# A fused block of attention and quantised feed-forward layers on one core: two VectorE operations, the seam between its halves, and its end are set to other places

## The reference, cut to what matters

```python
x = x + attn_a(layernorm(x))   # 16 heads, 64 wide; gelu; adds its own input too
x = x + ffn(layernorm(x))      # 256 -> 1024 -> relu -> 256, weights quantised to -1, 0, 1
x = x + attn_b(layernorm(x))   # 16 heads, 16 wide, rotary embedding, biases
x = x + ffn(layernorm(x))      # same weights
```

## Time and profile before

| what | us |
|---|---|
| median of 3 runs (3780.09 to 3784.66) | 3782.32 |
| profiled execution, its own time | 3781.21 |
| profiled execution, span from first to last instruction | 3779.0 |
| PE busy | 3626.6 |
| DVE busy | 2584.8 |
| ACT busy | 2385.9 |
| POOL busy | 1888.6 |

### The profile page before, as it was taken

How to read it: one execution, slowest core, us unless ns; L and a number is a source line. 1 busy time by engine, 2 the same in 40 slices (tenths; PEclk the granted TensorE clock), 3 DMA queues, 4 the chain that set the end, 5 groups by cost and what they waited for, 6 DMA issues and landing times.

```text
span 3779.0 us, 64440 instructions
## 1 busy us (share of the span) xinstructions
PE 3626.6 (96%) x23810; PEld 2433.1 (64%) x23810; DVE 2584.8 (68%) x4296; ACT 2385.9 (63%) x4629; POOL 1888.6 (50%) x1337
## 2 busy tenths in 40 slices
PE   8999999999999999999999978999999999999987
PEld 6777777777777777777777664555555555555534
DVE  6766666666667666666767656777777777777763
ACT  5665656556566566655656546777777777777754
POOL 4555555556555555555654633444444444444412
PEclk9999999999999999999999998999999999999989
DMA  2000000000000000000000012222222222222220
GB/s 79 7 12 1 12 12 12 1 12 12 1 12 12 1 12 12 9 5 12 12 1 15 25 43 47 53 62 62 63 62 61 61 63 58 62 59 64 53 48 18
DMA packets 102329, 116.27 MB, mean 31 GB/s; under 512 B 23557, under 2 KB 75269, under 8 KB 102021
## 3 DMA queue, kind: packets, MB, share of 16 engines
q1 hardware_dynamic: 102020, 112.17, 12.0%
HBM read 34.48 MB, written 27.26 MB: 16 GB/s over the span
## 4 chain that ended last, share of the span: by engine, by line
PE 76%; DVE 11%; ACT 7%; issue 5%; POOL 1%; DMA 0%; DVEq 0%; ACTq 0%; SPq 0%
PE ps_o L675 12%; PE ps_s L644 10%; PE ps_t L657 8%; PE ps_t L226 8%; PE ps_m L657 4%; PE ps_o L751 4%; PE ps_t L233 4%; DVE max_b L1160 4%; PE ps_t L786 4%; PE ps_m L226 3%; PE ps_t L710 3%; PE ps_s L724 3%; ACT et L867 2%; PE ps_m L233 2%; PE ps_s L738 2%
## 5 line engine op out<-in xcount | busy, mean ns | idle before, releaser
L534 POOL TENSOR_TENSOR e_a<-e_a,recip 128x1024 f32<-128x1024 f32 x512 | 969.4, 1894 | 948.7 <-DVE recip L1027 948.5
L825 ACT ACTIVATE e_a<-ps_s,neg_max 128x512 f32<-128x512 f32 x1024 | 695.1, 685 | 544.8 <-DVE neg_max L1020 544.4
L1160 DVE TENSOR_REDUCE max_b<-ps_s 128x2 f32<-128x1024 f32 x512 | 625.0, 1221 | 270.6 <-PE ps_s L724 268.8
L867 ACT ACTIVATE et<-ps_s 128x1024 f32<-128x1024 f32 x512 | 527.4, 1030 | 319.9 <-PE ps_s L738 319.0
L1020 DVE TENSOR_REDUCE neg_max<-ps_s 128x2 f32<-128x1024 f32 x512 | 623.0, 1217 | 67.7 <-PE ps_s L644 67.7
L675 PE MATMUL ps_o<-et_a,v_a 128*64 128x256 f32 x4096 | 499.8, 386 | 9.1 <-DVE heads_a L1063 4.8
L644 PE MATMUL ps_s<-raw_a 64*128 64x512 f32 x3072 | 425.9, 409 | 5.5 <-ACT e_a L825 5.3
L675 PEld LDWEIGHTS ps_o<-et_a,v_a 128*64 128x64 f32 x4096 | 279.2, 137 | 192.1 <-issue 78.3
L657 PE MATMUL ps_t<-ident,e_a 128*128 128x128 f32 x2660 | 394.0, 280 | 2.1 <-DVE xl L1219 2.0
L1034 DVE COPY et_a<-ps_t 128x512 f32<-128x512 f32 x366 | 251.1, 688 | 206.3 <-PE ps_t L657 202.1
L657 PEld LDWEIGHTS ps_t<-ident,e_a 128*128 128x128 f32 x2660 | 290.1, 141 | 133.2 <-issue 129.3
(11 more groups left out here) (194 smaller groups left out, 7231.0 us busy)
## 6 DMA issues: line engine op xcount, KB each, us to landing
q_stack<-roped_q SPq DMA_DIRECT2D x256, 96.0 KB
k_stack<-roped_k SPq DMA_DIRECT2D x256, 96.0 KB
x_a<-X SPq DMA_DIRECT2D x16, 512.0 KB, 3.4
X<-x_a SPq DMA_DIRECT2D x16, 512.0 KB, 2.9
x_ahead<-X SPq DMA_DIRECT2D x16, 512.0 KB, 3.8
X<-x_ahead SPq DMA_DIRECT2D x16, 512.0 KB, 2.9
x_before<-X SPq DMA_DIRECT2D x16, 512.0 KB, 3.9
OUT<-x_before SPq DMA_DIRECT2D x16, 512.0 KB, 5.2
```

What stands on the lines that cost most here:

```text
L534: nc.gpsimd.tensor_tensor(e_a[:, u % 5, :, :], e_a[:, u % 5, :, :], factor, ALU.mult).then_inc(e_normed, 1)
L825: ins = nc.scalar.activation(e_a[:, u % 5, h, :], ps_s[:, 2 * (u % 2) + h, :], ACT.Exp, bias=neg_max[:, u % 5, h:h + 1], accum_out=sums[:, ...
L867: nc.scalar.activation(et[:, v % 5, :, :], ps_s[:, 2:4, :], ACT.Exp)\
L1160: nc.vector.reduce_max(max_b[:, u // 4 % 2, :, u % 4], ps_s[:, score_bank(u):score_bank(u) + 2, :], AX.X, negate=True).then_inc(max_done, 1)
```

## The change: what it does

1. **Two VectorE operations, every sequence.** `LOWS[1]` (the second `roped_q`) goes from r = -26 to r = -24, behind the maximum of the next slot. In ffn1's norm the first `statistics` goes from r = 103 to 107, the second from 108 to 109, `aggregate` from 109 to 110. In the frame of one sequence, r = -24 is r = 104 of the sequence two before, so these stand side by side on DVE.
2. **End.** ffn1 of the last but one sequence (s = 14), with its output product, norm and bias, is set some 5 to 20 steps earlier, into the last scores of s = 15, and its save from r = 152 to r = 130.
3. **Seam.** x of sequence 1 goes to `x_before` instead of `x_ahead`; `load_second` loads it at slot 503, under a semaphore of its own, instead of after sequence 0's save. Its first norm and transposes are 4 to 12 steps earlier. The last heads' casts and low parts are two slots earlier, their product is at slots 528 and 529 instead of 536 to 538, in front of sequence 0's attn transposes, and the save of x is at 535 instead of 540.
4. **Transposes.** The first transpose of a norm waits for each 128-token piece of `xn` by itself and no longer for all four.

```diff
-        POST, LAST_POSTS = ((32, 32, 35, 36), (43, 44, 51, 52)), (56, 57, 58, 58)
+        POST, LAST_POSTS = ((32, 32, 35, 36), (43, 44, 51, 52)), (48, 48, 49, 49)
-        RESIDUAL, LOAD_X, SAVE_X, LAST_SAVE = 13, -22, 54, 60
+        RESIDUAL, LOAD_X, SAVE_X, LAST_SAVE = 13, -22, 54, 55
...
-                        if table[half][k] + late(s, half) == slot - UNITS * s:
+                        sooner = 2 if table is HEADS_HIGH and late(s, half) else 0
+                        if table[half][k] + late(s, half) - sooner == slot - UNITS * s:
...
-        NORM = {"ffn0": (-101, -100, -98, -93, -91), "attn": (-67, -64, -63, -51, -49), "ffn1": (103, 108, 109, 113, 115)}
+        NORM = {"ffn0": (-101, -100, -98, -93, -91), "attn": (-67, -64, -63, -51, -49), "ffn1": (107, 109, 110, 113, 115)}
+        WO_EARLY, XT_EARLY, FFN_EARLY = (95.5, 96.5, 98.5, 99.5), (107.1, 108.1), (99, 101, 102, 104, 105)
+        UP_EARLY, DOWN_EARLY = (110.1, 111, 112, 113.5, 115, 116.5, 118, 119), (121.5, 123.5, 125.5, 127)
+        BIAS_EARLY, SAVE_EARLY = 107, 130
+        XT_RAMP, FFN_RAMP = (-93.9, -92.9), (-109, -108, -107, -104, -103)
-        ROTATE, HIGHS, LOWS = (-39, -37, -35, -34, -32, -30), (-31, -29, -23, -21), (-28, -26, -20, -18)
+        ROTATE, HIGHS, LOWS = (-39, -37, -35, -34, -32, -30), (-31, -29, -23, -21), (-28, -24, -20, -18)
...
-        x_of = {"ffn0": x_ahead, "attn": x_ahead, "ffn1": x_before}
+        def x_of(part, s):
+            return x_before if part == "ffn1" or s == 1 else x_ahead
...
+                def load_second():
+                    sp.wait_ge(a_x_out, 16 * 2)
+                    sp.dma_start(x_before[:, :, :], X1[1, :, :].rearrange("(t p) d -> p t d", p=P)).then_inc(second_in, 16)
...
-                        pe.wait_ge(xn_ready, TB * (nth_norm[part, s] + 1))
                         for t in range(TB):
+                            if i == 0:
+                                pe.wait_ge(xn_ready, TB * nth_norm[part, s] + t + 1)
```

More of the change, by code:

```diff
@@ L158, in hybrid_block_kernel @@
         x_in = sem("x_in")
+        second_in = sem("second_in")
         a_x_out = sem("a_x_out")
@@ L320, in hybrid_block_kernel @@
         for s in range(BATCH):
-            plan += [(XT0[k], "transpose", "ffn0", k, s) for k in range(KT)]
+            plan += [((XT_RAMP if s == 1 else XT0)[k], "transpose", "ffn0", k, s) for k in range(KT)]
             plan += [((UP_RAMP if s == 1 else UP0)[f], "up", "ffn0", f, s) for f in range(FT)]
@@ L326, in hybrid_block_kernel @@
             plan += [(VB[t], "v", "attn", t, s) for t in range(TB)]
[L327 to L330, removed]
+            early = s == BATCH - 2
+            plan += [((WO_EARLY if early else WO1)[t], "wo", "ffn1", t, s) for t in range(TB)]
+            plan += [((XT_EARLY if early else XT1)[k], "transpose", "ffn1", k, s) for k in range(KT)]
+            plan += [((UP_EARLY if early else UP1)[f], "up", "ffn1", f, s) for f in range(FT)]
+            plan += [((DOWN_EARLY if early else DOWN1)[t], "down", "ffn1", t, s) for t in range(TB)]
         plan = sorted((SLOT * s + at_step, kind, part, i, s) for at_step, kind, part, i, s in plan)
@@ L354, in norm_at @@
         def norm_at(part, s):
-            return ATTN_RAMP if (part, s) == ("attn", 1) else NORM[part]
+            if (part, s) == ("ffn0", 1):
+                return FFN_RAMP
+            if (part, s) == ("attn", 1):
+                return ATTN_RAMP
+            return FFN_EARLY if (part, s) == ("ffn1", BATCH - 2) else NORM[part]
         norms = sorted((SLOT * s + norm_at(part, s)[0], part, s) for s in range(BATCH) for part in NORM)
@@ L434, in save_ahead @@
                     sp.wait_ge(biased, nth_norm["attn", s] + 1)
-                    sp.dma_start(X1[s, :, :].rearrange("(t p) d -> p t d", p=P), x_ahead[:, :, :]).then_inc(x_saved, 16)
+                    sp.dma_start(X1[s, :, :].rearrange("(t p) d -> p t d", p=P), x_of("attn", s)[:, :, :]).then_inc(x_saved, 16)
                 def load_before(s):
-                    sp.wait_ge(x_saved, 16 * (s + 1))
+                    sp.wait_ge(x_saved, 16 * max(s + 1, 2))
                     if s:
@@ L507, in _ @@
                         load_rest()
+                        load_second()
                     if slot == KEY_ONES:
@@ L512, in _ @@
                             r = step - SLOT * s
-                            if r == -108:
+                            if r == -108 and s != 1:
                                 load_ahead(s)
@@ L524, in _ @@
                                 load_before(s)
-                            if r == 152:
+                            if r == (SAVE_EARLY if s == BATCH - 2 else 152):
                                 save_before(s)
@@ L562, in add_bias @@
                         pool.wait_ge(weights_in, 8 * 16)
-                    nc.gpsimd.tensor_tensor(x_of[part][:, :, :], x_of[part][:, :, :],
+                    nc.gpsimd.tensor_tensor(x_of(part, s)[:, :, :], x_of(part, s)[:, :, :],
                                             rows_of(bo_rows if part == "attn" else b2_rows), ALU.add).then_inc(biased, 1)
@@ L620, in _ @@
                             for part in NORM:
-                                if r == BIAS[part]:
+                                if r == (BIAS_EARLY if (part, s) == ("ffn1", BATCH - 2) else BIAS[part]):
                                     add_bias(part, s)
@@ L874, in normalise @@
                     for t in (first, first + 1):
-                        nc.scalar.activation(xn[:, t, :], x_of[part][:, t, :], ACT.Identity, scale=rstd[:, t:t + 1],
+                        nc.scalar.activation(xn[:, t, :], x_of(part, s)[:, t, :], ACT.Identity, scale=rstd[:, t:t + 1],
                                              bias=shift[:, t:t + 1]).then_inc(xn_ready, 1)
@@ L1115, in statistics @@
                 def statistics(part, s, t):
-                    if part == "ffn0":
-                        dve.wait_ge(x_in, 16 * (s + 1))
+                    if part == "ffn0" and s == 1:
+                        dve.wait_ge(second_in, 16)
+                    elif part == "ffn0":
+                        dve.wait_ge(x_in, 16 * max(s, 1))
                     else:
@@ L1121, in statistics @@
                     for t in (t, t + 1):
-                        ins = nc.vector.bn_stats(stats[:, t, :], x_of[part][:, t, :])
+                        ins = nc.vector.bn_stats(stats[:, t, :], x_of(part, s)[:, t, :])
                     ins.then_inc(stats_ready, 1)
@@ L1135, in normalise @@
                     for t in (first, first + 1):
-                        nc.vector.tensor_scalar(xn[:, t, :], x_of[part][:, t, :], mean_var[:, t, 0:1], rstd[:, t:t + 1],
+                        nc.vector.tensor_scalar(xn[:, t, :], x_of(part, s)[:, t, :], mean_var[:, t, 0:1], rstd[:, t:t + 1],
                                                 ALU.subtract, ALU.mult).then_inc(xn_ready, 1)
@@ L1184, in empty @@
                         wait_filled(dve, fill)
-                        x = x_of[part][:, i - 1:i + 1, :]
+                        x = x_of(part, s)[:, i - 1:i + 1, :]
                         emptied(nc.vector.tensor_tensor(x, x, both, ALU.add), fill)
```

## The result

The kernel after takes 3836.9 us (median of 4 runs, 3833.8 to 3837.9), the kernel before, run beside it, 3783.5 us. The ratio is 1.014, 95% interval [1.0122, 1.0157]: 53 us slower, between 46 and 59. The forecast was 3805 us, 22 us slower: the sign was right, the size less than half.

What follows compares the result with a forecast made beforehand. TensorE, VectorE and ScalarE were taken to bound each sequence in turn, as a relay. 3781.2 + 29.5 (hold) + 4 (clock) - 8.3 (seam) - 2.0 (end) = 3804.4, plus 1.1 for the median: 3805.5 us; range 3774 to 3820.

Steps and rivals of the forecast that it cites:

- The held operation: Second `roped_q`, held on VectorE by GpSimd's ffn0 bias add: 2.11 us a sequence, 29.5 us over 14.
- the hold: Second `roped_q` ends at 3319.86, 0.55 us after GpSimd's add, instead of 3317.99: 1.87 us a sequence.
- the new place of `roped_q`: With `roped_q` moved away, VectorE waits for `xh` before `xl`: 0.24 us a sequence.
- The norm's later steps: ffn1's `statistics` and `aggregate` cost nothing new: power comes 1.1 us before `xn` needs it, VectorE being late.
- the relay: Within a sequence, whatever delays the last `roped_k` delays ScalarE's stretch, and TensorE's behind it, by the same amount.
- a port shared by halves: Alternative to full exclusion at `roped_q`: it loses another 0.6 us, 0.84 a sequence, 12 us in all.
- The clock: TensorE's idle time before the late maximum lowers the clock in about half of 13 sequences: 4 us, ends 0 and 21.
- the clock falls in every sequence: Rival: TensorE's doubled idle time lowers the clock in all 13 sequences, 21 us instead of 4: 3822; chance 0.05 above 3820.
- The seam: Last heads' products fill TensorE's idle time before the transposes; with 0.8 at sequence 1's norm, 8.3 us gained.
- The end: Twelve products moved into the last scores -0.3, x's earlier arrival -0.9, transposes -0.8: -2.0 us, ends -4.7 and +0.7.
- The sum: Whole kernel: 3781.2 + 29.5 + 4 - 8.3 - 2.0 = 3804.4, median 3805.5 us, 0.6% slower.

Runs made afterwards that it cites:

- the added products: Kernel after, with eight added 128x512 products per sequence where TensorE waits for the late maximum: 3818.5 us, ratio 1.0084.
- The three kernels with another end: Kernel before with the early end alone (3792.0 us), plus x in the other buffer (3786.4), plus two added products behind each of the last ten turned scores (3787.3).
- the two seam kernels: Kernel after with `LOWS`, `NORM` and end as before: 3785.6 us; the same with the last heads' low parts two slots earlier too: 3780.2 us.

## Why the prediction was right in sign and wrong in size

**The held operation: right.** The place (3317.40 for 3317.39), the duration (2.47 us, forecast 2.4 to 2.5), the end 0.55 us after GpSimd's, and the price once the clock is taken out (1.96 us a sequence, forecast 2.11) all hold. Term by term, the hold cost 1.75 us where 1.87 stood and the new place of `roped_q` 0.06 where 0.24 stood. The norm's later steps, which the prediction put at nothing because VectorE would be the late one at `xn`, cost 0.15: in that the reading failed, with GpSimd's power the late one. The runs with the add one step earlier and with `roped_q` back show it to be the cause. That the relay hands it on in full holds too; only the way is another, through TensorE's wait for the maximum and ScalarE's for scores.

The Trainium skill (SBUF — State Buffer, "Who interferes with whom") lets a VectorE instruction with two SBUF inputs and a GpSimd instruction that reads SBUF exclude each other. The trace agrees: 2.47 us beside the add, 0.68 us clear of it, where a port shared by halves would have given 1.2.

**The clock: the step that failed most.** The prediction said: "With more idle time I expect it in about half, at less than 1.6 us each", and took 4 us. The 2.4 us of idle time were forecast (2.36 measured), but not what they do: the clock fell in 13 of 13 sequences, at 1.22 us each, which is 15.9 us. The rival that had this, "the clock falls in every sequence", had the count right, with 1.6 us each, and gave 3822 us, still 15 short. What misled was one fall in 13 sequences, read as a chance of the edge to be scaled up. Eight falls in 13 with a hold of 2.05 us, 13 with 2.46 show how steeply it goes. The Trainium skill (TensorE: Matmul & The Clock Gate, "What's actually happening") lets the clock fall after idle time, and I named it for that rival; the falls came after TensorE's 2.36 us of idle time and 12 of 13 went when the added products left 0.51.

By traces, hold and clock make 14 x 1.96 + 13 x 1.22 = 43.3 us, and from the second `roped_q` of sequence 1 to that of sequence 15 the kernel after takes 43.6 us more than the kernel before. The two timed kernels that differ in `roped_q` alone are 45 us apart by their medians and 48 by their ratios. What lies between is within what such a difference is uncertain by.

**The seam: wrong.** "Their input is there in time ... casts and low parts need four operations of 1.3 us" failed. I counted four operations and did not place them: the casts move, the low parts do not, and the fourth stands behind the power in GpSimd's queue. The forecast was -8.3 us; measured are +1.1 (-2.3 to +4.5). With the low parts moved it is -5.3. Why it is not -8.3 stays open. Counted from the same `h_lo` in front of the seam (2201.67 before, 2204.70 with the low parts moved), the transposes start only 0.3 us later than before, so the idle time did take the four products. But the first stacked keys leave 3.4 us earlier, where 7.5 were forecast.

**The end: wrong in sign.** -2.0 us forecast, +7.2 measured (3.8 to 10.2), above the upper end of +0.7. The step said that x "no longer arrives at 3744.5 behind a load of 5.05 us" and looked at the load of s = 15 only. The earlier output product of s = 14 needs a load too, and that one waits for a save out of its buffer: 5.7 us of the 7.2 went with the other buffer. The low clock of the last slots was in the forecast, and was there (0.63 of full). How much of the 5.7 us is the clock, and what it costs by itself, the runs do not part.

**The sum.** Hold and clock +43 to +48 where 33.5 stood, seam +1 where -8.3 stood, end +7 where -2.0 stood: each of the three terms missed by 9 to 15 us and all to the same side. The single kernels add up to 56 us, the change is 53.

## What to carry to other kernels

When an operation with two SBUF inputs is moved, look up what GpSimd does at its new minute and which of the two could go first; here one step of a bias add was worth 43 us. Count the idle time that a delay leaves on TensorE, for that can cost more than half of the delay again (1.22 us on 1.96). And when work is pulled forward, follow every input of it by queue, casts, low parts and loads, to the instruction ahead of it: twice here the product was early and its input was not.

## What the runs showed of the hardware

- The same 2.4 us of idle time on TensorE, every 95.57 us, brought a fall to 1.2 GHz of some 3.4 us in 13 of 13 sequences, each time just as the work came back. With the 1.11 us of before it came in one of 13 as well, and with 0.51 us of idle time in one of 13. Eight added products of 2.20 us in all made the kernel 18 us faster.
- Which of two engines is held can hang on a few hundredths of a microsecond. In all 13 sequences of the kernel with added products GpSimd's `h_lo` started 0.02 to 0.04 us behind the third `xn`. In 11 of them the `xn` took 0.37 us, in the two with the shortest distance 1.46 us, and those two sequences were 1.1 us longer.
- Executions of the same instructions differ at the seam. The three kernels with another end have the code of before up to 3.6 ms; in their traces the first maximum of sequence 1 comes 3.4, 5.6 and 3.4 us later than in the trace of before. The traces of the two seam kernels differ by 2.66 us in front of anything that their edit moves; the later one has two stretches at the low clock there that the other lacks. So a seam is judged by timed rounds, and two traces are compared there only from an operation in front of it on.
